# Token mixing as products of 64 rows instead of 128, in a kernel of four residual layers

## What is computed

```python
x = x + L0(x)   # attention over a paged cache with a window of 256 tokens, 8 query heads, 4 key heads, then Wo
x = x + L1(x)   # token mixing: each sequence's 64 tokens by one of 8 matrices
x = x + L2(x)   # W_base, and a low-rank adapter chosen for each sequence
x = x + L3(x)   # W, and a low-rank adapter chosen for each sequence

def L1(x, subjects, weights):         # weights: 8 x 64 x 64
    w = weights[subjects]             # one 64 x 64 matrix for each sequence
    return einsum('bct,bcd->bdt', x, w)
```

## Time and profile before

| | |
|---|---|
| median of 3 runs | 459.99 us |
| lowest and highest | 459.63, 460.76 us |
| span of the profiled execution | 503.1 us |
| TensorE busy, products | 450.7 us (90%) |
| TensorE busy, loads | 326.4 us (65%) |
| VectorE busy | 302.0 us (60%) |
| GpSimd busy | 267.9 us (53%) |
| ScalarE busy | 229.6 us (46%) |

### The profile page before, as it was taken

One profiled execution on the slowest core, in us unless ns is written; L12 is line 12 of the kernel. 1 busy time (PEld: TensorE's weight loads), 2 busy tenths in 40 slices (PEclk: granted clock), 3 DMA queues, 4 the chain that ended last, 5 costly groups with the idle time before them and its releaser, 6 DMA issues.

```text
span 503.1 us, 9985 instructions
## 1 busy us (share of the span) xinstructions
PE 450.7 (90%) x2890; PEld 326.4 (65%) x2890; DVE 302.0 (60%) x869; ACT 229.6 (46%) x590; POOL 267.9 (53%) x241
## 2 busy tenths in 40 slices
PE   5999997799797899898989898999999998979997
PEld 2444467455476677585857676777677766857776
DVE  4988873375464466464756565665656475756542
ACT  1322112343564365454555564555555555555541
POOL 2588166446665546565665656657565655654000
PEclk9999997799998989999999999999999999999999
DMA  6385867837335665545455554645454545444111
GB/s 195 104 303 193 287 186 202 261 99 245 85 110 125 172 166 134 140 105 167 104 154 153 140 166 126 166 123 169 111 166 108 170 108 144 116 138 118 49 55 43
DMA packets 80731, 74.29 MB, mean 148 GB/s; under 512 B 51012, under 2 KB 57284, under 8 KB 80678
## 3 DMA queue, kind: packets, MB, share of 16 engines
q1 hardware_dynamic: 61712, 47.22, 32.6%
q0 software_dynamic: 15456, 22.08, 16.5%
q10 hardware_dynamic: 3510, 4.35, 2.4%
HBM read 83.59 MB, written 11.93 MB: 190 GB/s over the span
## 4 chain that ended last, share of the span: by engine, by line
PE 61%; DVE 9%; issue 8%; SPq 6%; DMA 6%; ACT 5%; another core or an unknown queue 4%; ACTq 0%; DVEq 0%
PE banks L1104 23%; PE banks L1235 7%; PE banks L1241 6%; PE banks L1117 6%; PE banks L1268 5%; PE banks L1253 4%; PE banks L1098 4%; PE banks L1217 2%; DMA mask<-masks_dram 2%; DMA stage<-wo_dram 2%; DVE prob L974 2%; DVE x L892 2%; PE banks L1281 1%; ACT x L667 1%
## 5 line engine op out<-in xcount | busy, mean ns | idle before, releaser
L519 POOL DMA_INDIRECT windows<-kvrows_dram,idx_all x78 | 82.1, 1053 | 64.8 <-PE banks L1253 29.2
L639 ACT ACTIVATE pt_s<-banks 112x384 f32<-112x384 f32 x128 | 57.5, 498 | 88.5 <-PE banks L1241 67.6
L519 POOL DMA_INDIRECT windows<-newkv,idx_all x78 | 78.8, 1011 | 29.4 <-issue 21.9
L633 ACT ACTIVATE prob<-prob,negmax 128x336 f32<-128x336 f32 x128 | 72.2, 565 | 37.9 <-DVE negmax L974 21.5
L974 DVE CUSTOM_DVE_ANT_0 prob<-banks,mask 128x336 f32<-128x336 f32 x128 | 58.6, 505 | 47.7 <-issue 25.8
L489 POOL TENSOR_TENSOR rstd<-ms,half 128x8 f32<-128x8 f32 x24 | 46.3, 1928 | 72.6 <-DVE ms L912 52.3
L1117 PE MATMUL banks<-wkv_s,xt_s 128*128 128x512 f32 x128 | 59.1, 617 | 6.0 <-DMA xt_s<-xt_dram 5.2
L1235 PE MATMUL banks<-kt_s,qt_s 64*128 64x336 f32 x256 | 50.2, 482 | 4.9 <-ACT kt_s L627 3.4
L1241 PE MATMUL banks<-cst,prob 128*112 128x128 f32 x384 | 53.4, 275 | 0.0
L1104 PE MATMUL banks<-wf_hi,x 128*128 128x512 f32 x120 | 42.1, 412 | 10.0 <-DVE x L892 8.6
L984 DVE TENSOR_SCALAR prob<-prob,rinv 128x336 f32<-128x336 f32 x128 | 49.0, 425 | 2.3
(11 more groups left out here) (211 smaller groups left out, 821.3 us busy)
## 6 DMA issues: line engine op xcount, KB each, us to landing
usel<-utab SPq DMA_DIRECT2D x64, 128.0 KB
xt_s<-xt_dram SPq DMA_DIRECT2D x31, 256.0 KB
mask<-masks_dram SPq DMA_DIRECT2D x32, 168.0 KB
newkv<-kvo SPq DMA_DIRECT2D x16, 256.0 KB, 3.5
stage<-xtok_dram SPq DMA_DIRECT2D x16, 256.0 KB
tsel<-ttab SPq DMA_DIRECT2D x64, 64.0 KB
out_dram<-xo ACTq DMA_DIRECT2D x15, 256.0 KB
windows<-kvrows_dram,idx_all POOLq DMA_INDIRECT x78
```

Source lines behind the costliest of these rows:

```text
L519: P.indirect_dma_start(kv_s[i][:, c, :], None, newkv if new else kvrows, bass.IndirectOffsetOnAxis(ap=idx_all[:, new * CH + c, b:b + 1], a ...
L633: A.activation(pr, pr, ACT.Exp, bias=negmax[:, g:g + 1], scale=-1.0, accum_out=psum_p[b % 2][:, g:g + 1]).then_inc(S["exp_done"], 1)
L639: A.activation(pt_s[g][:], tb[g % 2][0:KP, 0:CH * 128].rearrange("p (c q) -> p c q", c=CH), ACT.Copy).then_inc(S["pt_ev"], 1)
```

## The change

`mix` makes eight products in place of four: for each chunk of features, one for each sequence of the tile. A product takes 64 tokens of `x1` (64 rows, 128 stationary columns) with the sequence's own 64 x 64 matrix (64 moving columns). The first sequence's four results go to the first 256 columns of one bank, the second's to those of the next bank. These two are `sbk[3]` and `gb`, which get neighbouring physical numbers 6 and 7; `bank` and `kpair` are numbered anew so that all other names keep their roles. Since `sbk[3]` holds scores until VectorE has read them, `mix` waits for `negs_ready` at 4b + 4 as well, with b = k, before its two other waits. ScalarE's and VectorE's instructions on the result read both banks, in an order by sequence.

```diff
-        bank = [banks[:, i] for i in range(8)]
+        bank = [banks[:, i] for i in (0, 1, 5, 6, 2, 3, 4, 7)]
...
+        def mixed():
+
+            return banks[:, 6:8, 0:256].rearrange("p u (c t) -> p u c t", c=C)
+
+        def by_sequence(x):
+
+            return x.rearrange("p c (u t) -> p u c t", u=2)
+
         def kpair(i):
 
-            return banks[:, 2 * (i % 3):2 * (i % 3) + 2]
+            first = (0, 5, 2)[i % 3]
+            return banks[:, first:first + 2]
...
-                A.activation(x2_s[0], gb[:].rearrange("p (c t) -> p c t", c=C), ACT.Copy).then_inc(S["x2_hi"], 1)
+                A.activation(by_sequence(x2_s[0]), mixed(), ACT.Copy).then_inc(S["x2_hi"], 1)
...
-                low(x2_s[0], x2_s[1], gb[:].rearrange("p (c t) -> p c t", c=C), "x2_hi", t + 1, "x2_lo")
+                low(by_sequence(x2_s[0]), by_sequence(x2_s[1]), mixed(), "x2_hi", t + 1, "x2_lo")
...
-            def mix(t):
+            def mix(t, b):
+                pe.wait_ge(S["negs_ready"], 4 * b + 4)
                 pe.wait_ge(S["x1_ready"], t + 1)
                 pe.wait_ge(l_w1[t % 2], 32 * (t // 2 + 1))
                 for c in range(C):
-                    last = mm(gb[:, 128 * c:128 * c + 128], x1[:, 128 * c:128 * c + 128], w1i[t % 2][:], start=True, stop=True)
+                    for u in range(2):
+                        own = slice(64 * u, 64 * u + 64)
+                        last = mm(mixed()[:, u, c], x1[own, 128 * c:128 * c + 128], w1i[t % 2][own, own], start=True, stop=True)
                 last.then_inc(S["l1_mm"], 1)
...
-                        mix(t - 1)
+                        mix(t - 1, k)
```

## The result

| | before | after |
|---|---|---|
| median of 20 runs | 457.25 us | 459.81 us |
| lowest and highest | 454.98, 460.76 us | 456.68, 463.05 us |
| ratio, 95% interval | | 1.006 (1.0038 to 1.0083) |
| span of the profiled execution | 503.1 us | 454.6 us |

The change makes the kernel slower, by 2.7 us as the ratio has it (1.7 to 3.8). The median of before over 20 runs is 2.7 us lower than that of the three runs of which the prediction knew.

A forecast was written before the change was run, and what follows sets the result against it. The prediction took TensorE to bound the loop over tiles. It summed 15 x (0.15 border + 0.02 wait) + 0.26 for one late tile = 2.8 us, onto 459.99: 462.8 us, range 461.4 to 465 (chance 0.60).

The forecast's parts named there:

- The level it was set against: Time of the whole kernel before, 459.99 us, to which the forecast change of 2.8 us was added.
- absorbed: Rival: query transposes shift inside TensorE's gap ahead of `base`, so the delay vanishes; 459.8 to 460.7 us, chance 0.20.
- TensorE bounds the loop, and the 43 us are late signals: Loop over tiles: TensorE-bound; profiled span's excess over the timed 459.99 us is mostly late signals, about 2 us per tile.
- The step is paced by the load of 128 stationary columns: Mixing: halving moving columns gains nothing per step, still 0.112 us; only the last product ends 0.053 us sooner.
- Halves run in pairs: Mixing: row halves load and run side by side, eight steps of 0.112 us, plus 0.007 for a pair's second.
- The rival that runs them in a row: Mixing: the halves' 16 loads go one after the other, +0.97 us per tile, 475.1 us; chance 0.08.
- The border: Mixing to query transposes: shape change costs 0.095 and a bare load 0.10; the whole way 1.14 against 0.99, +0.15 us per tile.
- The wait: Ahead of the mixing: waiting for the fourth score reduction costs +0.02 us per tile, bounds 0 and 0.06.
- The number of tiles: Sum over the loop: the per-tile cost of 0.15 + 0.02 us was counted 15 times.
- The late tile: Second tile, with late reductions: the mixing no longer fills TensorE's wait, 0.26 us more, once.
- ScalarE, VectorE and the banks cost nothing: Copy and subtraction after the mixing, and renumbered banks: same columns in another order, no added time.
- Half the time for half the columns: Rival: mixing steps paced by columns, 0.056 in place of 0.112 us, -0.28 us per tile, 456.1 us; chance 0.07.

The follow-up runs named there:

- the second trace of before: The kernel before, unchanged, profiled once more; span 455.4 us, one run at 457.51 us, a tile 20.66 us.
- banks_only: The kernel before with only the new numbers of the banks; ratio to before 1.0011 (0.9982 to 1.0039).
- wait_only: The kernel before with only the new wait of the mixing for the fourth reduction; ratio to before 1.0006 (0.9971 to 1.0041).
- one_half: The changed kernel with only the first sequence's four mixing products per tile, output not the reference's; ratio to before 1.0045 (1.0018 to 1.0072).
- narrow_full: The kernel before with 64 moving columns in the mixing and all 128 rows, half the result left out; a tile 20.60 us.
- column_halves: The kernel before with the mixing cut by stationary columns into eight products of 128 rows, 64 columns; one run 460.22 us, undisturbed tile 20.58 us.
- quadrants: The changed kernel with each mixing product cut again by stationary columns, sixteen of 64 rows and 64 columns; ratio to before 0.9997 (0.9968 to 1.0026).

## Why the prediction was right and wrong, point by point

**The level it was set against: wrong, and this made the number wrong.** "459.99 + 2.8 = 462.8" rests on the median of three runs. Twenty runs have 457.25, and they scatter from 454.98 to 460.76; the three (459.63 to 460.76) all lay in the upper part. Set against 457.25, the 462.8 is a change of 5.55 us, where the medians differ by 2.56. With 457.25 as the level the same sum gives 460.1, 0.3 from the measured 459.81; the change itself was forecast at 2.8 us and measured at 2.7 (1.7 to 3.8). The wrong level also puts the measured time in the wrong place: 459.81 is not in the forecast's 461.4 to 465 but at the lower edge of the 459.8 to 460.7 of "absorbed", a rival whose mechanism did not happen.

Where the scatter comes from is in part known. From the third mixing to the fourteenth the undisturbed tiles of one kernel are equal to 0.02 us. The way to the third varies: it starts at 188.2 in the second trace of before, at 188.7 in banks_only, at 189.5 in wait_only and at 186.1 in after. Of this the smaller part is the late tile. The first mixing starts at 137.6, 139.4, 138.5 and 135.6 in these traces, and from there to the third it is 50.6, 49.3, 51.0 and 50.4. What varies ahead of the first mixing no run looked into.

**TensorE bounds the loop, and the 43 us are late signals: right.** Tiles of 20.66 us, TensorE busy in all of them but the late one, and ScalarE's copy follows the mixing in 0.04 us and not 1.19. The "2 us of gaps" of the first trace are not in the timed program.

**The step is paced by the load of 128 stationary columns: right.** Steps of 0.112 with 64 moving columns, in after, in one_half and in narrow_full; eight more cost 0.90. Loads of 64 columns (quarters) make it 0.058. The four shapes of this case fit together: 128 stationary columns 0.112, with 128 or 64 moving ones; 64 stationary and 128 moving 0.108, near the 0.107 that the prediction has for 128 moving columns; 64 and 64 0.058. In these four the larger of the two numbers of columns sets the step.

**Halves run in pairs: right.** Half the products take as long as all of them. The rival that runs them in a row would have cost 0.8 us more per tile.

**The border: right in its place, mis-sized.** I had 0.15 us for it and the traces give 0.10. This is the term of the sum per tile that was off. From the first record to the first working transpose I summed to 1.14; it is 1.04 + 0.055 = 1.10. Three terms are off: the second pair starts 0.16 after the first, not 0.215 (narrow_full has the same 0.16 with 128 rows); the last pair holds the array for a full step, not for its 0.053 of columns, so from its start to the transposes it is 0.20 and not 0.15; and the bare load behind it costs 0.055 and not 0.10, since the second transpose starts 207.86 + 0.44 - 0.272 = 208.03 and a step there is 0.11.

**The wait: right in the steady tiles**, 0.02 us each, alone and in the change. So a tile costs 0.12 where I had 0.17.

**The number of tiles: off.** I took 15 times the cost. The tile with the late mask absorbs what comes before it, so 13 tiles count, 13 x 0.116 = 1.5 (0.116 is the difference of the two quotients above before rounding), and the late tile itself.

**The late tile: right that the mixing moves behind the wait, its size about a quarter of what it was.** I had 0.26 us, with the mixing at its usual 1.04; the term left out that the clock may be low there. In the trace that I had, TensorE waited 2.96 us in that tile and the mixing ran ahead of the wait. In after (timelines of DVE and PE, and the busy times of the stretch of low clock, columns as in the table of two tiles):

```profile
163.13 0.09 DVE L983 DVE_READ_ACCUMULATOR2_ANT negmax<- 128x1 f32 x1
...
163.27 1.97 PE L1280 MATMUL banks<-w1i,x 64*128 64x64 f32 x16 [6.85 <-DVE negmax L983]
165.17 1.11 PE L1139 MATMUL banks<-cst,qrot 128*128 128x128 f32 x4
...
160.70:167.50 6.80, 4.23 (x28) 4.11 (x29) 4.82 (x16) 4.01 (x12) 4.36 (x4) 0.50 0.52 131
```

TensorE has been idle for 6.85 us, and the granted clock is at 0.50, the level of 1.2 GHz, until 167.5. The mixing and its border take 1.90 us there in place of 1.04. In the second trace of before the clock falls too (0.50 from 163.3 to 170.1), but its mixing had run at 158.23, ahead of the wait, at the full clock in 1.16. From the end of the last reduction to the transposes it is 166.34 to 167.01, 0.67 us, before, and 163.22 to 165.17, 1.95, after. Part of this comes back, since the clock rises sooner behind the transposes; from the last reduction to the next mixing it is 188.21 - 166.34 = 21.87 and 186.05 - 163.22 = 22.83. By this pair of traces the late tile costs 0.96 us. Other traces show how much that can vary. With the mixing ahead of the wait the way is again 21.9 in banks_only and 21.8 in column_halves, but 23.0 in narrow_full, where the clock stays at 0.50 for 10.2 us and not for 6.8. With the mixing behind the wait it is 23.1 in wait_only (10.3 us at 0.50) and 23.8 in one_half. So the term is about 1 us by one pair of traces; over all of them it can be anything from nothing to 2 us. With 1.0 the sum by the traces is 1.5 + 1.0 = 2.5 us, inside the measured 1.7 to 3.8. That my 2.8 came so near the 2.7 is in part luck: the tiles cost less than I had and the late one more, and the two errors cancel. With the masks asked for early, all 15 tiles count and none is late; 15 x 0.116 = 1.7 us is what the two kernels then differ by.

**ScalarE, VectorE and the banks cost nothing: right** as far as can be seen, a median of 0.599 us for the copy before and 0.597 after, and 1.0011 for the banks alone.

**The rivals.** "Absorbed" did not happen, though the margin ahead of `base` is as thin as stated. "Half the time for half the columns" fell in narrow_full. Its idea comes back with the quarters, where the load too is half as wide. No rival named the masks, though the view of waits of the first trace has a row in which VectorE waits 4.3 us for one.

## What to carry to other kernels

Halving the rows or the moving columns of small products does not help while each needs a load of 128 stationary columns: find which of load and columns sets the step, cut that one, and count what each change of shape costs with the neighbours ahead and behind. A forecast in microseconds is only as good as the level that it is added to: three runs put it 2.7 us too high here, as much as the change is worth. Before a change of some tenths of a microsecond per tile, take a second trace and more runs, and look for what stands out in them; here one transfer, asked for too late by the order of its queue, was worth four times as much as the change, and it had to go first for a better product to show. A transfer that lands with a margin of one or two microseconds can be late in the next execution: from request to landing the same mask took 12.7 to 16.5 us here. And a wait put ahead of work in place of behind it can move that work into a stretch of low clock, so ask of the tiles that stall and not only of the steady ones.

## What the runs showed that I had not expected

The same program gave profiled spans of 503.1 and 455.4 us; in the first, ScalarE's copy came 1.0 to 1.6 us behind the end of the mixing in 13 of 15 tiles, in the second 0.04 us in 14, and the timed runs are like the second. A mask of 168 KB takes 11 to 15 us from request to its last part in the steady part of the loop, with the transfer engines busy for 0.61 of the time, and up to 16.5 us in quadrants; its first part is there after 2 to 4 us. At the end of a wait of 7 us on TensorE the granted clock is 0.50, and the work moved behind that wait takes nearly twice as long (the mixing 1.97 us in place of 1.11). Quarters of 64 rows and 64 columns run four at a time, 0.007 us behind one another, and such groups of four follow each other at 0.058 us, where pairs of halves take 0.112.
